# A two-network transformer block on one core: earlier weight pieces, split key-query product, and one output bank finished ahead of the scales of tile 2

## What is computed

```python
def fp4_quant_dequant(x):                      # blocks of 16 along the last dimension
    xb = x.reshape(shape[:-1] + (shape[-1] // 16, 16))
    scale = maximum(max(abs(xb), axis=-1, keepdims=True) / 6.0, 1e-12)
    q = _GRID[searchsorted(_MID, abs(xb / scale))] * sign(xb) * scale
def _L0_ffn_ref(x, w_gate, w_up, w_down):      # w_gate, w_up: 704 x 256, w_down: 256 x 704
    h = silu(fp4_linear(x, w_gate)) * fp4_linear(x, w_up)
    return fp4_linear(h, w_down)               # fp4_linear quantises both operands
x = x + 0.5 * ffn(layernorm(x))                # the first network
x = x + attention(layernorm(x), Wq, bq, Wk, bk, Wv, bv, Wo, bo)
x = x + 0.5 * ffn(layernorm(x))                # the second network, same weights
```

## Time and profile before

| | us |
|---|---|
| median of three runs | 943.67 (943.57 to 944.26) |
| profiled execution, whole | 942.09 |
| its span, first to last instruction | 940.3 |
| TensorE busy | 908.0 (97%) |
| VectorE busy | 707.4 (75%) |
| ScalarE busy | 652.2 (69%) |
| GpSimd busy | 498.0 (53%) |

### The profile page before, as it was taken

One profiled execution on the slowest core, in us unless ns is written; L12 is line 12 of the kernel. 1 busy time (PEld: TensorE's weight loads), 2 busy tenths in 40 slices (PEclk: granted clock), 3 DMA queues, 4 the chain that ended last, 5 costly groups with the idle time before them and its releaser, 6 DMA issues.

```text
span 940.3 us, 16317 instructions
## 1 busy us (share of the span) xinstructions
PE 908.0 (97%) x5704; PEld 811.5 (86%) x5704; DVE 707.4 (75%) x1163; ACT 652.2 (69%) x1368; POOL 498.0 (53%) x557
## 2 busy tenths in 40 slices
PE   3899999999999999999999999999998999999997
PEld 2778888888988799989998899998998988989887
DVE  7988988898777666655574544545598899999997
ACT  6677788888885475767675576767783777656554
POOL 3555677666630064535663064546577656756562
PEclk9999999999999999999999999999999999999999
DMA  9100000000000000000000000000000000000001
GB/s 319 48 1 1 1 1 1 2 1 1 1 1 2 1 1 1 1 1 2 1 1 1 1 1 1 1 2 1 1 1 1 1 24 24 23 23 24 5 20 45
DMA packets 11553, 13.83 MB, mean 15 GB/s; under 512 B 848, under 2 KB 10576, under 8 KB 11472
## 3 DMA queue, kind: packets, MB, share of 16 engines
q1 hardware_dynamic: 11472, 12.79, 4.1%
HBM read 8.59 MB, written 4.19 MB: 14 GB/s over the span
## 4 chain that ended last, share of the span: by engine, by line
PE 82%; DVE 9%; issue 3%; POOL 3%; ACT 3%; DMA 0%; SPq 0%; DVEq 0%; ACTq 0%; POOLq 0%
PE bank L1707 21%; PE bank L1945 18%; PE bank L1610 6%; PE bank_b L1718 6%; PE bank_b L1725 4%; PE bank L1983 4%; PE bank L1987 4%; PE bank L1985 4%; PE bank L1908 2%; PE bank L1746 2%; PE bank_b L1987 1%; PE bank_b L1983 1%; PE bank_b L1985 1%; POOL p_lo L553 1%; PE bank L1926 1%
## 5 line engine op out<-in xcount | busy, mean ns | idle before, releaser
L553 POOL TENSOR_TENSOR p_lo<-s_ring,p_hi 128x512 fp32r<-128x512 f32 x128 | 168.4, 1320 | 219.8 <-ACT p_hi L1469 219.7
L515 POOL TENSOR_TENSOR zq<-grid,s_neg 128x256 f32<-128x256 f32 (+2 forms) x184 | 173.3, 966 | 42.1 <-DVE grid L752 39.8
L913 DVE TENSOR_TENSOR top<-bank,top 128x512 f32<-128x512 f32 x112 | 77.4, 691 | 125.8 <-ACT s_ring L1453 125.7
L1707 PE MATMUL bank<-w_hi,T_hi 128*128 128x512 f32 (+1 forms) x384 | 150.6, 392 | 3.4 <-DVE z L711 2.5
L1707 PE MATMUL bank<-w_hi,T_lo 128*128 128x512 f32 (+1 forms) x384 | 144.9, 377 | 0.0
L1707 PE MATMUL bank<-w_lo,T_hi 128*128 128x512 f32 (+1 forms) x384 | 144.4, 376 | 0.0
L1453 ACT ACTIVATE s_ring<-bank 128x512 f32<-128x512 f32 x128 | 75.9, 593 | 78.0 <-PE bank L1945 77.9
L1292 ACT ACTIVATE T_hi<-bank 128x1024 fp32r<-128x1024 f32 (+1 forms) x68 | 64.6, 950 | 83.8 <-PE bank L1610 83.8
L1983 PE MATMUL bank<-v_hl,p_hi 128*128 128x258 f32 x384 | 109.9, 286 | 0.5 <-DVE x L945 0.3
L1987 PE MATMUL bank<-v_hl,p_lo 128*128 128x258 f32 x384 | 108.2, 282 | 0.0
L1985 PE MATMUL bank<-v_hl,p_hi 128*128 128x256 f32 x384 | 108.2, 282 | 0.0
(11 more groups left out here) (223 smaller groups left out, 2288.5 us busy)
## 6 DMA issues: line engine op xcount, KB each, us to landing
out<-x SPq DMA_DIRECT2D x7, 512.0 KB, 2.9
x<-in_L_attn_hidden_states SPq DMA_DIRECT2D x3, 1024.0 KB, 14.3
x<-in_L_attn_hidden_states SPq DMA_DIRECT2D x2, 512.0 KB, 7.4
wraw<-in_L_ffn_w_down SPq DMA_DIRECT2D x1, 704.0 KB, 8.2
wraw<-in_L_ffn_w_gate SPq DMA_DIRECT2D x1, 640.0 KB, 4.4
wraw<-in_L_ffn_w_up SPq DMA_DIRECT2D x1, 640.0 KB, 6.1
wq_s<-in_L_attn_Wq SPq DMA_DIRECT2D x1, 512.0 KB, 8.2
wk_s<-in_L_attn_Wk SPq DMA_DIRECT2D x1, 512.0 KB, 9.2
```

The source lines that it names most:

```text
L515: last = nc.gpsimd.tensor_tensor(out=blocks(zq[:, to:to + hi - lo]), in0=blocks(grid[:, lo:hi]), in1=spread(s_neg[:, par, lo // BLOCK:hi / ...
L553: nc.gpsimd.tensor_tensor(out=lower_buf(n, c), in0=score_buf(n, c), in1=upper_buf(n, c).bitcast(F32), op=ALU.subtract).then_inc(plo_done, 1)
L913: nc.vector.tensor_tensor(out=top[:], in0=score_bank(c), in1=other, op=ALU.max).then_inc(top_done, 1)
L1707: last = nc.tensor.matmul(gu[:, lo:hi], lhsT=T[:, par, HK + kd, :], rhs=w[:, kd, lo:hi], start=n == 0, stop=n == len(terms) - 1)
```

## The change

Four parts, of which the first three lie in the first ramp.

1. **Weight pieces.** The gate weights come in two transfers (three tiles, then two and the mixed tile), so that piece 0 waits for the first alone. The scales of pieces 0 and 1 are computed apart. The scaled pieces 1, 2 and 5 are computed by GpSimd (`weight_y` in its list) and no longer by VectorE. VectorE's and ScalarE's lists are put in another order, among it the grid of piece 4 behind the first product, and the statistics of input tiles behind the products of tiles 1 and 2; GpSimd's quantised pieces 4 and 5 stand together behind a wait for the first `y_done`.
2. **Key-query product.** `wq` and `wk` are issued ahead of the second part of x. Its second half (four matmuls) is spread between the transposes of the weight groups, and its split comes later.
3. **Query bias.** 12 products with a single column (24 passes) are replaced by one row product (four matmuls, 257 columns) in round -2, a copy by ScalarE, and three single-column products in round -1.
4. **The joint.** `finish_last` does its first bank ahead of `scales(2, 0)` and the other three behind it; ScalarE's list has `chain_rest(-1, 1)` behind two `p_upper`.

The diff, cut to its core:

```diff
@@ SyncE
-            sp.dma_start(wraw[:, 0:5 * D].rearrange("p (j d) -> p j d", d=D),
-                         w_gate[0:5 * P, :].rearrange("(j p) d -> p j d", p=P)).then_inc(gate_in, 16)
-            sp.dma_start(wraw[0:HR, 5 * D:6 * D], w_gate[5 * P:I, :]).then_inc(gate_in, 16)
-            sp.dma_start(wraw[HR:P, 5 * D:6 * D], w_up[0:P - HR, :]).then_inc(gate_in, 16)
+            sp.dma_start(wraw[:, 0:3 * D].rearrange("p (j d) -> p j d", d=D),
+                         w_gate[0:3 * P, :].rearrange("(j p) d -> p j d", p=P)).then_inc(gate_in, 16)
+            sp.dma_start(wraw[:, 3 * D:5 * D].rearrange("p (j d) -> p j d", d=D),
+                         w_gate[3 * P:5 * P, :].rearrange("(j p) d -> p j d", p=P)).then_inc(mixed_in, 16)
+            sp.dma_start(wraw[0:HR, 5 * D:6 * D], w_gate[5 * P:I, :]).then_inc(mixed_in, 16)
+            sp.dma_start(wraw[HR:P, 5 * D:6 * D], w_up[0:P - HR, :]).then_inc(mixed_in, 16)
...
             load_x(0)
+            sp.dma_start(wq_s[:], rows_of(wq)).then_inc(qk_in, 16)
+            sp.dma_start(wk_s[:, :, 0:D], rows_of(wk)).then_inc(qk_in, 16)
             load_x(1)
-            sp.dma_start(wq_s[:], rows_of(wq)).then_inc(qk_in, 16)
-            sp.dma_start(wk_s[:], rows_of(wk)).then_inc(qk_in, 16)
@@ GpSimd
+            def weight_y(i):
+                pool.wait_ge(wc["inv"], SCALED[i])
+                if i >= 2:
+                    pool.wait_ge(wc["abs"], i - 1)
+                    pool.wait_ge(wc["rnd"], i - 1)
+                nc.gpsimd.tensor_tensor(out=blocks(wy[:, i % 2, :]), in0=blocks(wraw[:, i * I:(i + 1) * I]),
+                                        in1=spread(wsm[:, 3, i * HB:(i + 1) * HB], HB),
+                                        op=ALU.mult).then_inc(wc["y_pool"], 1)
+            weight_y(1)
             weight_q(0)
+            weight_y(2)
+            weight_q(1)
             group_std(0)
-            for i in (1, 2, 3):
-                weight_q(i)
+            weight_q(2)
+            weight_q(3)
             first_ffn(-5, 1)
             broadcast_biases()
             first_ffn(-4, 0)
-            weight_q(4)
-            first_ffn(-3, 1)
+            pool.wait_ge(wc["y"], 3)
+            weight_y(5)
             group_std(1)
+            first_ffn(-3, 1)
+            first_ffn(-2, 0)
+            pool.wait_ge(y_done, 1)
+            weight_q(4)
             weight_q(5)
-            ffn_rounds(first_ffn, -2)
+            ffn_rounds(first_ffn, -1)
@@ VectorE, first ramp
-            dve.wait_ge(gate_in, 16 * 3)
-            weight_scales(1, 0, 2)
+            dve.wait_ge(gate_in, 16)
+            weight_scales(1, 0, 1)
             weight_y(0)
-            weight_y(1)
+            dve.wait_ge(mixed_in, 16 * 3)
+            weight_scales(2, 1, 2)
             weight_grid(0)
             dve.wait_ge(up_in, 16)
-            weight_scales(2, 2, 4)
+            weight_scales(3, 2, 4)
             weight_grid(1)
-            weight_y(2)
             weight_y(3)
             weight_grid(2)
+            weight_grid(3)
             first_blocks(-6, 0)
-            weight_grid(3)
             first_blocks(-5, 1)
             dve.wait_ge(wd_in, 16)
-            weight_scales(3, 4, NW)
+            weight_scales(4, 4, NW)
+            first_blocks(-4, 0)
             weight_y(4)
-            first_blocks(-4, 0)
+            first_product(0)
             weight_grid(4)
-            first_product(0)
-            weight_y(5)
             first_blocks(-3, 1)
@@ VectorE, rounds: statistics behind the product while c is negative
                     blocks_of(c, par)
-                    if f == 0:
+                    if f == 0 and c >= 0:
                         input_statistics(c)
                     if hidden(c + 3):
                         product(c + 3)
+                    if f == 0 and c < 0:
+                        input_statistics(c)
@@ VectorE, joint
             to_grid(1)
+            finish_last(0)
             scales(2, 0)
-            finish_last()
+            finish_last(1, 2, 3)
@@ ScalarE, first ramp
             weight_abs(1)
             x_means(0)
             x_variances(0)
-            x_means(1)
             weight_abs(2)
             weight_abs(3)
-            normalise(0)
-            m_upper()
             upper_group(0)
             upper_group(1)
+            normalise(0)
...
             chain_rest(-4, 0)
-            normalise(2)
             absolute(-3)
-            weight_abs(4)
+            m_lower()
+            normalise(2)
+            x_means(1)
+            silu_gate(0)
             normalise(3)
             absolute(-2)
-            silu_gate(0)
             chain_upper(-3, 1)
-            query_bias()
-            woT_out(0)
+            weight_abs(4)
             chain_rest(-3, 1)
             x_variances(1)
+            weight_abs(5)
+            woT_out(0)
             woT_out(1)
-            weight_abs(5)
             normalise(4)
@@ TensorE
             key_query_product()
+            key_query_rest(0)
             transpose_group(0)
             transpose_group(1)
+            key_query_rest(1)
             weight_lower(0)
             weight_lower(1)
-            key_query_lower()
+            key_query_rest(2)
             transpose_group(2)
             transpose_group(3)
+            key_query_rest(3)
             weight_lower(2)
             weight_lower(3)
+            key_query_lower()
...
             transpose_wo(0)
-            query_bias()
             chain_lower(0, -3, 1)
-            pe.wait_ge(aw["bq_s"], 2)
             transpose_wo(1)
@@ TensorE, rounds -2 and -1
                     if extra and c == -2:
+                        pe.wait_ge(aw["woT_s"], 2)
+                        query_row()
                         value_output_product(0)
                     if extra and c == -1:
+                        query_bias()
                         value_output_lower()
```

More of the change, by code:

```diff
@@ L958, in finish, with finish_last @@
                 new_x(n, QT - 1)
-            def finish_last():
+            def finish_last(*which):
                 n = NQ - 1
-                for i, a in enumerate(LAST_ORDER):
+                for i in which:
+                    a = LAST_ORDER[i]
                     if i == 0:
@@ L1331, in step @@
                     extra = f == 0
-                    if chain(c + 1) and (f or not last(c + 1)):
+                    if chain(c + 1) and (f or not last(c + 1)) and (f or c != -1):
                         absolute(c + 1)
@@ L1360, in step @@
                         absolute(NT - 1)
+                    if extra and c == -2:
+                        query_row()
                     if chain(c) and not late(c):
@@ L1623, in key_query_product, with key_query_rest @@
                 pe.wait_ge(qk_in, 16 * 2)
-                for dt in range(KD):
-                    last = product(m_bank[:, dt * D:(dt + 1) * D], wq_s[:, :, dt * P:(dt + 1) * P], wk_s, dt == 0)
-                last.then_inc(aw["m"], 1)
+                product(m_bank[:, 0:D], wq_s[:, :, 0:P], wk_s[:, :, 0:D])
+            def key_query_rest(j):
+                last = nc.tensor.matmul(m_bank[:, D:2 * D], lhsT=wq_s[:, j, P:2 * P], rhs=wk_s[:, j, 0:D],
+                                        start=False, stop=j == KE - 1, skip_group_check=True)
+                if j == KE - 1:
+                    last.then_inc(aw["m"], 1)
             def key_query_lower():
@@ L1632, in key_query_lower, with query_row @@
                                  stop=True, skip_group_check=True).then_inc(aw["m_sub"], 1)
+            def query_row():
+                pe.wait_ge(aw["bk"], 1)
+                product(bank2[0:1, 0, 0:D + 1], b3[:, 0, :].unsqueeze(2),
+                        wk_s[:, :, 0:D + 1]).then_inc(aw["row"], 1)
             def query_bias():
-                pe.wait_ge(aw["bcast"], 1)
-                bq_col = b3[:, 0, :].unsqueeze(2)
-                product(bq_sum[:, 0:1], bkB, bq_col)
-                for e in range(KD):
-                    last = product(bq_sum[:, 1 + e:2 + e], wk_s[:, :, e * P:(e + 1) * P], bq_col)
+                pe.wait_ge(aw["row_s"], 1)
+                one = ident[0:1, 0:1]
+                cols = [bq_row[:, D:D + 1].to_broadcast([1, P])] + [bq_row[:, e * P:(e + 1) * P] for e in range(KD)]
+                for n, col in enumerate(cols):
+                    last = nc.tensor.matmul(bq_sum[:, n:n + 1], lhsT=col, rhs=one, start=n == 0, stop=True,
+                                            skip_group_check=True)
                 last.then_inc(aw["bq"], 1)
@@ L1880, in _ @@
             pe.wait_ge(wc["lo"], G1)
+            pe.wait_ge(lo_done, number_lo(0, -4))
+            gate_up(0, 0)
+            gate_up(0, 1)
             pe.wait_ge(aw["m_lo"], 1)
-            pe.wait_ge(lo_done, number_lo(0, -4))
-            for columns in range(3):
-                gate_up(0, columns)
+            gate_up(0, 2)
             transpose_chain(0, -3)
             transpose_wo(0)
-            query_bias()
```

(1 more changed line is left out.)

45 lines of the change are left out of this document (31 added, 14 removed).

## The result

| | before | after |
|---|---|---|
| median, us | 943.96 (943.57 to 944.58, 4 runs) | 934.75 (933.85 to 934.96, 4 runs) |
| profiled execution / its span, us | 942.09 / 940.3 | 933.85 / 932.0 |

What follows compares the result with a forecast made beforehand. The prediction took VectorE to bound the first ramp and, at the joint, TensorE's gap waiting for VectorE's update, with half clock behind it. Ramp -4.0 and joint -3.5 gave -7.5: 943.67 to 936.2 us, range 934.4 to 940.2.

Steps and rivals of the forecast that it cites:

- the low end: Fast end of the forecast range: ramp -5.3 us and joint -3.9 us, written as 934.4 us.
- Start of VectorE: Ramp: VectorE starts once three gate tiles are in, not all gate and mixed tiles; -1.3 us from 5.94.
- Product of tile 0: Ramp, VectorE: five terms (-1.3, -1.6, +0.6, -1.7, +0.8) sum to -3.2 us, so it starts at about 31.8, not 35.04.
- The single prices (scaled pieces, grid, silu): Ramp, VectorE's walk: scaled pieces 1 and 2 gone -1.6 us, grid of piece 4 later -1.7, silu behind four means +0.8.
- `gate_up` of tile 1: Ramp, TensorE: held by ScalarE's split of tile -3 until about 33.8, against 37.14 before; -3.3 us.
- From there to `gate_up` of tile 3: Ramp, TensorE: `gate_up` and transposes to 38.1, then row +1.6, columns +0.3, value-output +5.1, rest +6.8; 51.9 against 55.85.
- VectorE's product of tile 2: Ramp: starts at 49.8 instead of 54.83, ends at 50.7, 1.2 us before TensorE needs it.
- Who sets the ramp: Ramp, 6 to 56 us: everybody waits for VectorE, directly or through ScalarE and GpSimd; VectorE works 47.44 of 50 us.
- The ramp's clock: Ramp, TensorE: half clock at 38 us follows the bias's single-column products; without them `gate_up` of tile 1 takes 3.9 + 0.2.
- GpSimd's multiplies: Ramp: three new multiplies charged nothing for collisions with VectorE; pieces 4 and 5, about 3.9 us, over before about 49.
- The joint: Start of the second network: update 1.9 us earlier, gap 2.62 to 0.7, full clock behind it 1.7; -3.5 us altogether.
- The slower rival: Ramp: idle 2.2 us near 21 to 23 brings half clock through three `gate_up`, costing 10.8 us: 947.0; 8% with similar mishaps.

Runs made afterwards that it cites:

- e6: The changed kernel with the gate weights in one transfer, so VectorE's first scales wait for gate and mixed tiles as before: 936.25 us, ratio 0.9935 to the kernel before.
- e7: The changed kernel with scaled pieces 1, 2 and 5 back on VectorE: 938.05 us, ratio 0.9950 to the kernel before.
- e8: The changed kernel with the grid of piece 4 ahead of the product of tile 0, as before: 937.47 us, ratio 0.9955 to the kernel before.
- e5: The changed kernel with the query bias in its old place and form (12 single-column products, 24 passes): 937.98 us, ratio 0.9955 to the kernel before.
- e4: The kernel before with 22 transposes of the identity into unused PSUM put in TensorE's gap at the joint: 941.42 us against 943.16, ratio 0.9984.
- e1: The kernel before with only finish_last divided, its first bank ahead of the scales of tile 2: 940.36 us against 943.16, ratio 0.9972.
- e2: The kernel before with both joint edits (finish_last divided, chain_rest(-1, 1) behind two p_upper): 940.11 us against 943.16, ratio 0.9965.
- e3: The changed kernel with both joint edits undone, so the ramp's changes alone: 937.59 us against 943.16 for the kernel before, ratio 0.9944.
- e9: The changed kernel again, unaltered, as yardstick on the chip of later variants: 933.96 us, ratio 0.9902 to the kernel before.
- e11: The changed kernel with the bias row product and its copies moved forward, into TensorE's gap ahead of group 2's lowering: 935.05 us, ratio 0.9911 to the kernel before.

## Why the prediction was right

The time is inside the range, 1.5 us below the number by the medians and 0.8 by the profiled executions (933.85 where 934.6 was written). It is inside by little: the low end, 943.67 - 5.3 - 3.9 = 934.5 (934.4 was written), is a gain of 9.2 us, and 9.2 were measured. The mechanism of the joint was right. In the ramp the steps that were named do win, but several terms were mis-sized in ways that cancel, and the engine that was named as the limit is the limit only in the first part. Point by point:

- **Start of VectorE**: forecast 1.3 earlier, found 1.70 (4.24), and at 4.22 to 4.33 in every trace with the gate divided. In the traces with the whole gate it is 5.84 to 6.83, where VectorE waits for the last of three transfers. That it arrives in full is shown by e6.
- **Product of tile 0**: forecast 31.8, found 31.27, but not by the sum that was written. That sum walks VectorE's list, and in its row the product waits 0.69 us for TensorE's `gate_up` of tile 0: VectorE was ready at 30.58, so its terms were worth 4.5 us and not 3.2, and a wait that the sum did not hold gave 0.7 back. The single prices (scaled pieces, grid, silu) were not measured one by one: undone singly they cost more than they were priced, the scaled pieces by their collision with GpSimd and a gap grown from 2.01 to 2.62 us (e7), the grid by a wait of 2.16 us (e8).
- **`gate_up` of tile 1**: forecast 33.8, found 32.98. I had the split of tile -3 on ScalarE as what holds it. It ends at 32.92, and the last transposes of `wo` end within 0.02 of that, so this trace can't tell which of the two releases `gate_up`; in e5 it is the split, with a wait of 0.20 us. The step was right and its size 0.8 too long.

```profile
32.54 0.38 ACT L1342 ACTIVATE T_lo<-bank 128x256 fp32r<-128x256 f32 x1
```

- **From there to `gate_up` of tile 3**: forecast 18.1 us, found 17.99, by errors that cancel. To the row product 4.79 (forecast 4.3, with 0.32 for tile -2's quantised part), row product 1.83 (1.6), single columns 0.75 (0.3), value-output 4.12 (5.1, which held a wait of 0.78 us for ScalarE that the three columns now cover; the largest single error on TensorE's side), the rest 6.50 (6.8). The end is 50.97 where 51.9 was written.
- **VectorE's product of tile 2**: forecast 49.8, found 49.48. It ends 0.6 us before TensorE wants it; I had 1.2.
- **Who sets the ramp**: I wrote that VectorE is what everybody waits for. That fits the kernel before. In the changed kernel the last chain passes from VectorE to ScalarE at 21.8 and from 37.4 on it is mostly TensorE's. That less work on VectorE alone between 22 and 50 us would now win little is argued from this chain; no run tests it.
- **The ramp's clock**: the outcome was right (1.00 from 24 to 50), the reason is not shown. I put the fall at 38 us down to the single-column products. In all four traces with the ramp of before the clock falls either during the last of these passes (e4, at 36) or within 2 us behind them (the kernel before, e1 and e2, at 37 to 38); in e5, one trace, the same passes are followed by no fall. So the passes alone do not suffice, and whether they take part stays open. In e4 it fell a second time at 49 to 53.
- **GpSimd's multiplies**: pieces 4 and 5 together take 3.7 us (42.44 to 46.17; 3.9 forecast) and are over before the transposes at 48.48. Three scaled pieces on GpSimd are a gain: e7. Charging nothing for them was nearly right: GpSimd's own multiply at 14.56 lost 0.5 us to VectorE's scaled piece, and `s_up` at 44.67 lost 0.86 to piece 5.
- **The joint**: the gap fell by 2.30 us (forecast 1.9; the other 0.4 to 0.5 is the order of `p_upper`, which I had only in the bound) and the clock gave 1.59 (1.7, and shown by e4). But 0.70 were given back: from 718.26 to 722.22 TensorE needs 3.96 us where it needed 3.26, because VectorE's product of tile 3 now comes last there, with its wait of 0.40 us. 2.30 + 1.59 - 0.70 = 3.19; forecast 3.5. That VectorE would bind behind `project_down` I did not see. The rows of TensorE in the kernel before to which this bullet and the one on the value-output stretch compare:

```profile
47.36 0.47 PE L1663 MATMUL bank_b<-nv,neg_ident 128*128 128x512 f32 x1 [0.78 <-ACT nv L1197]
...
730.58 0.40 PE L1707 MATMUL bank<-w_hi,T_hi 128*128 128x512 f32 x1
```

- **The slower rival**, half clock behind the new gap near 22: in e3, with the same ramp lists as the changed kernel, it happened. That the first trace has none is luck.

```profile
22.96 0.79 PE L1730 MATMUL bank_b<-w_hi,neg_ident 128*128 128x512 f32 x1 [2.02 <-ACT w_hi L1165]
```

```profile
23.00:24.00 1.00, 1.00 (x2) 0.60 (x3) 0.93 (x5) 1.00 (x3) 1.00 (x3) 0.50 1.10 347
```

The gap is 2.02 us in e3 and 2.01 in the changed kernel; one falls, the other does not. It lasts 3 to 4 us and the ramp ends 0.92 us later (51.89). So the mechanism is real, and its size (10.8 us) was over-estimated more than ten times: in no trace did it last through three `gate_up`. The executions of the changed kernel divide likewise: one of 933.85 with a mean clock of 1.000, three of 934.67 to 934.96 with 0.998. In which of the waits those three fell no trace shows; in e9 four of the five have 1.000.

## What to carry to other kernels

A wait removed at the bottleneck can be worth its length and more on top by the clock (2.3 and 1.6 us at the joint); see what clock the stretch behind it has, and price both. In a ramp with hand-written lists, undoing one part of a good order measures that part and the waits that it opens, so single undoings (4.0, 2.3, 4.1 and 3.5 us by the medians here) do not add up to the whole ramp (4.9 in the trace, 5.6 by e3); the two parts that sit over 600 us apart do. When you price an undoing, look at more than one execution: the traced one was the longest of its kernel in e5 and in e7. And a long wait is not yet a cost: 12 us of TensorE at the start were free to grow by 1.9, because ScalarE and VectorE decide when the next thing can begin. Last, when the binding engine is relieved, follow the chain again: here it moved from VectorE to ScalarE and TensorE.

## What the runs showed of the hardware

- **The half clock is not a function of the instruction list.** The same ramp list fell at 23 us in e3 and nowhere in the first trace and in e9. In the traces it stood behind every gap of TensorE from 2.24 to 2.64 us: 2.62 (joint of before), 2.64 (joint of e3), 2.62 (e7), 2.56 (e8), 2.25 (e5) and 2.24 (e6). Of the gap ahead of group 2 it stood behind 2.02 (e3) and 1.99 (e5), but not behind 2.01 (first trace) and 2.02 (e9). It also stood behind 1.41 (e11) and 0.91 (e4, at 49), but not behind 1.57 (e8, at 23) or 1.48 (the kernel before, at 24), and in the ramp of before it came near 36 to 38 behind no gap of a microsecond. Whether the other executions fell at the same places is not known. Most stretches lasted 3 to 4 us, that of e7 over 6; those that could be priced cost 0.9 to 2 us.
- **Transposes kept it up.** In e4 TensorE did nothing but 22 transposes for 2.56 us at the joint, and the clock during and behind them was 1.00.
- **VectorE and GpSimd in turn.** GpSimd's multiply of 704 columns takes 1.39 us in most places (at 8.36, 10.21 and 30.65, say). At 14.56 it took 1.90, beginning while VectorE's scaled piece of 14.33 ran. VectorE's `s_up` of 60 columns took 1.08 us at 44.67, beside the multiply of piece 5 that GpSimd had begun at 44.29 (1.39 us), where it takes 0.22 at 39.24.

```profile
14.33 0.88 DVE L695 TENSOR_TENSOR wy<-wraw,wsm 128x704 f32<-128x704 f32 x1
14.56 1.90 POOL L470 TENSOR_TENSOR wraw<-wgrid,wsm 128x704 f32<-128x704 f32 x1 [0.53 <-DVE wgrid L711]
44.67 1.08 DVE L751 SCALAR_TENSOR_TENSOR s_up<-amax,c_up 128x60 f32<-128x60 f32 x1
```

The Trainium skill (SBUF — State Buffer, "Who interferes with whom") has a VectorE instruction with two SBUF inputs and a GpSimd instruction that reads SBUF exclude each other by a lock on a shared port pair. These rows agree in both directions: `s_up` ends at 45.75, just behind the multiply's 45.68.
